# Second feed-forward product in 25 blocks of 128 tokens instead of 32 items of 100

## What is computed

```python
def _qlinear(x, W, b):
    xq, sx, zx = _affine_quantize(x)          # min and max of all of x
    wq, sw = _sym_quantize(W)
    acc = jnp.einsum('bsh,oh->bso', xq - zx, wq)
    return acc * (sx * sw) + b
h = _qlinear(x, W1, b1)                       # 256 -> 1024
h = jax.nn.gelu(h, approximate=False)
out = _qlinear(h, W2, b2)                     # 1024 -> 256
...
x = x + _L0_xattn_ref(_layernorm(x), ctx_1024, ctx_1024, WQ, WK, WV, WO, mask)
x = x + _L0_ffn_ref(_layernorm(x), W1, b1, W2, b2)
```

## Time and profile before

| what | value |
|---|---|
| median of 3 runs | 1148.35 us (1147.01 to 1148.54) |
| the profiled execution, its time | 1149.17 us |
| the profiled execution, its span | 1147.3 us |
| PE busy | 1028.6 us, 90% of the span |
| DVE busy | 984.7 us, 86% |
| ACT busy | 871.5 us, 76% |
| POOL busy | 767.8 us, 67% |
| tail: first matmul of line 1261 to the end of the span | 1113.51 to 1147.3 us |

### The profile page before, as it was taken

One profiled execution on the slowest core, in us unless ns is written; L12 is line 12 of the kernel. 1 busy time (PEld: TensorE's weight loads), 2 busy tenths in 40 slices (PEclk: granted clock), 3 DMA queues, 4 the chain that ended last, 5 costly groups with the idle time before them and its releaser, 6 DMA issues.

```text
span 1147.3 us, 37568 instructions
## 1 busy us (share of the span) xinstructions
PE 1028.6 (90%) x10545; PEld 655.0 (57%) x10545; DVE 984.7 (86%) x2539; ACT 871.5 (76%) x1809; POOL 767.8 (67%) x1103
## 2 busy tenths in 40 slices
PE   4996899999999999999999999999999999975628
PEld 2553466666666666666666666666666666653318
DVE  5775899999999999999999999999999999965987
ACT  4652888888888888888888888888888888855824
POOL 2234677777777777777777777777777777764500
PEclk9998999999999999999999999999999999986959
DMA  8300576666666666666666666666666666664003
GB/s 258 94 1 18 100 136 132 132 133 133 133 133 133 133 133 133 133 133 133 133 132 132 132 132 132 132 132 132 132 132 132 132 132 132 132 128 127 1 0 116
DMA packets 441299, 138.22 MB, mean 120 GB/s; under 512 B 413556, under 2 KB 440252, under 8 KB 441276
## 3 DMA queue, kind: packets, MB, share of 16 engines
q1 hardware_dynamic: 441276, 137.93, 57.5%
HBM read 28.57 MB, written 6.55 MB: 31 GB/s over the span
## 4 chain that ended last, share of the span: by engine, by line
PE 73%; DVE 10%; ACT 6%; issue 4%; POOL 4%; DMA 1%; DVEq 1%; ACTq 0%; SPq 0%; POOLq 0%
PE front L337 18%; PE front L338 16%; PE front L339 16%; PE back L1196 8%; PE front L1178 6%; PE tp L1178 5%; POOL hl L571 3%; DVE hrange L1038 2%; DVE hrange L1039 2%; ACT prob L679 2%; DVE prob L914 2%; PE front L1261 1%; DVE k_l L934 1%; ACT q_h L721 1%; ACT ctx_h L713 1%
## 5 line engine op out<-in xcount | busy, mean ns | idle before, releaser
L571 POOL TENSOR_TENSOR hl<-prob,hl 100x361 f16<-100x361 f32 x512 | 432.7, 855 | 106.2 <-ACT hl L685 54.2
L679 ACT ACTIVATE prob<-prob,nmax 100x361 f32<-100x361 f32 x512 | 293.9, 586 | 46.8 <-DVE nmax L914 46.6
L337 PE MATMUL front<-ctx_h,wk_h 128*128 128x362 f16 x512 | 165.0, 322 | 42.2 <-DVE k_l L934 21.9
L1196 PEld LDWEIGHTS back<-v,pT 128*128 128x128 f16 (+1 forms) x4608 | 165.0, 98 | 45.7 <-issue 9.3
L685 ACT ACTIVATE hl<-prob 100x361 f16<-100x361 f32 x352 | 176.0, 500 | 7.9
L1196 PE MATMUL back<-v,pT 128*128 128x65 f16 (+1 forms) x4608 | 174.1, 194 | 7.0 <-DMA pT<-hl 7.0
L339 PE MATMUL front<-ctx_h,wk_l 128*128 128x362 f16 x512 | 162.4, 317 | 0.0
L338 PE MATMUL front<-ctx_l,wk_h 128*128 128x362 f16 x512 | 162.2, 317 | 0.0
L689 ACT ACTIVATE k_h<-front 128x362 f16<-128x362 f32 x256 | 118.9, 465 | 56.2 <-PE front L339 56.1
L934 DVE SCALAR_TENSOR_TENSOR k_l<-front,k_h 128x362 f16<-128x362 f32 x256 | 135.0, 528 | 27.9 <-ACT k_h L689 25.1
L914 DVE CUSTOM_DVE_ANT_0 prob<-front,mask_g,ngain 100x361 f32<-100x361 f32 x256 | 149.6, 584 | 2.9 <-PE front L1178 0.6
(11 more groups left out here) (180 smaller groups left out, 2011.6 us busy)
## 6 DMA issues: line engine op xcount, KB each, us to landing
ctx_raw<-ctxT SPq DMA_DIRECT2D x33, 361.0 KB, 3.2
pT<-hl SPq DMA_TRANSPOSE x256, 3.6
xs<-x SPq DMA_DIRECT2D x8, 400.0 KB
q_all<-x SPq DMA_DIRECT2D x32, 100.0 KB
out<-q_all SPq DMA_DIRECT2D x32, 100.0 KB
xb<-out SPq DMA_DIRECT2D x8, 400.0 KB
out<-xb SPq DMA_DIRECT2D x32, 100.0 KB
q_all<-wq SPq DMA_DIRECT2D x1, 1024.0 KB, 6.6
```

Of the source, the lines that this page charges most:

```text
L337: eng.matmul(dst, lh, rh, start=first, stop=False)
L571: pool.tensor_tensor(hl[0:T, n % RT, 1, 0:S], prob[0:T, n % RP, 0:S], hl[0:T, n % RT, 0, 0:S], ALU.subtract).then_inc(s_lo, 1)
L679: act.activation(prob[0:T, n % RP, 0:S], prob[0:T, n % RP, 0:S], ACT.Exp, bias=nmax[0:T, n:n + 1], scale=-1.0).then_inc(s_exp, 1)
L1196: ins = pe.matmul(obank[j % 2][:, n % GH * DV:(n % GH + 1) * DV], pT[0:r, n % RT, part_ * ST + st, :], v2[half][0:r, st, v, n % HT, :], st ...
```

## The change

The second product, the residual and the output no longer go item by item. All 3200 tokens are one row, cut into `NT` = 25 blocks of 128 tokens, which cross the boundaries of items.

```diff
+NT = B * T // P
+NX = 5
+CD = 3
-    hq = place("hq", [P, NB, NF, TW], F16)
+    hq = place("hq", [P, NF, B * T], F16)
-    xb2 = place("xb2", [P, B, D], F32)
+    xb2 = place("xb2", [P, NT, D], F32)
+    def blocks_of(c):
+        return [n for n in range(NT) if (n * P + P - 1) // TW == c]
+    def tokens(w):
+        return w.rearrange("b t d -> (b t) d").rearrange("(n p) d -> p n d", p=P)
...
         sp.dma_start(b2r[0:T, :], b2).then_inc(s_b12, 16)
+        sp.dma_start(b2r[T:P, :], b2[0:P - T, :]).then_inc(s_b12, 16)
...
-        for c in range(NB):
-            sp.dma_start(xb2[0:T, c * TB:(c + 1) * TB, :],
-                         out[c * TB:(c + 1) * TB].rearrange("b t d -> t b d")).then_inc(s_xi, 16)
-        for b in range(B):
-            sp.wait_ge(s_o, b + 1)
-            sp.dma_start(out[b], xb2[0:T, b, :]).then_inc(s_out, 16)
+        for c in range(NX):
+            ns = slice(c * NT // NX, (c + 1) * NT // NX)
+            sp.dma_start(xb2[:, ns, :], tokens(out)[:, ns, :]).then_inc(s_xi, 16)
+        for n in range(NT):
+            sp.wait_ge(s_o, n + 1)
+            sp.dma_start(tokens(out)[:, n, :], xb2[:, n, :]).then_inc(s_out, 16)
...
-        for c in range(NB):
-            x1 = xb2[0:T, c * TB:(c + 1) * TB, :]
-            pool.tensor_tensor(x1, x1, b2r[0:T, :].unsqueeze(1).broadcast_to([T, TB, D]), ALU.add).then_inc(s_xb, 1)
+        for c in range(NX):
+            x1 = xb2[:, c * NT // NX:(c + 1) * NT // NX, :]
+            pool.tensor_tensor(x1, x1, b2r[:, :].unsqueeze(1).broadcast_to([P, NT // NX, D]), ALU.add).then_inc(s_xb, 1)
...
-        for c in range(NB):
+        for c in [c for c in range(NB) if c != CD]:
             ts = slice(0, TW // 2 if c == 0 else TW)
-            act.activation(hq[:, c, :, ts].bitcast(I16), hid[:, c, :, ts], ACT.Identity,
+            act.activation(hq[:, :, c * TW + ts.start:c * TW + ts.stop].bitcast(I16), hid[:, c, :, ts], ACT.Identity,
...
-            for b in range(c * TB, (c + 1) * TB):
-                dve.wait_ge(s_f2, b + 1)
-                dve.scalar_tensor_tensor(out=xb2[0:T, b, :], in0=obanks[b % 8][0:T, 0:D], scalar=sc[0:T, S2:S2 + 1],
-                                         in1=xb2[0:T, b, :], op0=ALU.mult, op1=ALU.add).then_inc(s_o, 1)
+            for n in blocks_of(c):
+                dve.wait_ge(s_f2, n + 1)
+                dve.scalar_tensor_tensor(out=xb2[:, n, :], in0=obanks[n % 8][:, 0:D], scalar=sc[:, S2:S2 + 1],
+                                         in1=xb2[:, n, :], op0=ALU.mult, op1=ALU.add).then_inc(s_o, 1)
...
         for c in range(1, NB):
-            dve.wait_ge(s_h1, c + 1)
+            if c == CD:
+                dve.wait_ge(s_hd, 3)
+            else:
+                dve.wait_ge(s_h1, c + 1 - int(c > CD))
             h_codes(c, slice(0, TW))
+            if c == 1:
+                h_ints(CD, slice(0, TW))
             if c >= 2:
                 outputs(c - 2)
...
-                pe.wait_ge(s_hq, i // 2 + 1 if c == 0 else c + 2)
-                if b >= 8:
-                    pe.wait_ge(s_o, b - 7)
-                for m in range(NF):
-                    ins = pe.matmul(obanks[b % 8][0:T, 0:D], hq[:, c, m, i * T:(i + 1) * T], w2q[:, m, :],
+        for n in range(NT):
+            last = n * P + P - 1
+            pe.wait_ge(s_hq, last // TW + 2 if last >= TW // 2 else 1)
+            if n >= 8:
+                pe.wait_ge(s_o, n - 7)
+            for m in range(NF):
+                ins = pe.matmul(obanks[n % 8][:, 0:D], hq[:, m, n * P:(n + 1) * P], w2q[:, m, :],
```

More of the change, by code:

```diff
@@ L495, in _ @@
         sp.wait_ge(s_xo, 16 * B)
-        for c in range(NB):
-            sp.dma_start(xb2[0:T, c * TB:(c + 1) * TB, :],
-                         out[c * TB:(c + 1) * TB].rearrange("b t d -> t b d")).then_inc(s_xi, 16)
-        for b in range(B):
-            sp.wait_ge(s_o, b + 1)
-            sp.dma_start(out[b], xb2[0:T, b, :]).then_inc(s_out, 16)
-        sp.wait_ge(s_out, 16 * B)
+        for c in range(NX):
[4 more added lines that the diff above has]
+            sp.dma_start(tokens(out)[:, n, :], xb2[:, n, :]).then_inc(s_out, 16)
+        sp.wait_ge(s_out, 16 * NT)
     @block.gpsimd
@@ L608, in _ @@
                                ALU.max).then_inc(s_yp, 1)
-        pool.wait_ge(s_b12, 32)
-        pool.wait_ge(s_xi, 16 * NB)
-        for c in range(NB):
-            x1 = xb2[0:T, c * TB:(c + 1) * TB, :]
-            pool.tensor_tensor(x1, x1, b2r[0:T, :].unsqueeze(1).broadcast_to([T, TB, D]), ALU.add).then_inc(s_xb, 1)
+        pool.wait_ge(s_b12, 48)
+        pool.wait_ge(s_xi, 16 * NX)
+        for c in range(NX):
+            x1 = xb2[:, c * NT // NX:(c + 1) * NT // NX, :]
+            pool.tensor_tensor(x1, x1, b2r[:, :].unsqueeze(1).broadcast_to([P, NT // NX, D]), ALU.add).then_inc(s_xb, 1)
     @block.scalar
@@ L1044, in h_codes, with h_ints @@
         def h_codes(c, ts):
-            h = hq[:, c, :, ts]
+            h = hq[:, :, c * TW + ts.start:c * TW + ts.stop]
             dve.tensor_scalar(h, h.bitcast(I16), col(LO2), col(HI2), ALU.max, ALU.min).then_inc(s_hq, 1)
         def outputs(c):
-            for b in range(c * TB, (c + 1) * TB):
-                dve.wait_ge(s_f2, b + 1)
-                dve.scalar_tensor_tensor(out=xb2[0:T, b, :], in0=obanks[b % 8][0:T, 0:D], scalar=sc[0:T, S2:S2 + 1],
-                                         in1=xb2[0:T, b, :], op0=ALU.mult, op1=ALU.add).then_inc(s_o, 1)
+            for n in blocks_of(c):
+                dve.wait_ge(s_f2, n + 1)
+                dve.scalar_tensor_tensor(out=xb2[:, n, :], in0=obanks[n % 8][:, 0:D], scalar=sc[:, S2:S2 + 1],
+                                         in1=xb2[:, n, :], op0=ALU.mult, op1=ALU.add).then_inc(s_o, 1)
         first, second = slice(0, TW // 2), slice(TW // 2, TW)
-        dve.tensor_scalar(hq[:, 0, :, second].bitcast(I16), hid[:, 0, :, second], col(INV2), None,
-                          ALU.mult).then_inc(s_hd, 1)
+        def h_ints(c, ts):
+            dve.tensor_scalar(hq[:, :, c * TW + ts.start:c * TW + ts.stop].bitcast(I16), hid[:, c, :, ts], col(INV2), None,
+                              ALU.mult).then_inc(s_hd, 1)
+        h_ints(0, second)
         dve.wait_ge(s_h1, 1)
@@ L1061, in _ @@
         dve.tensor_tensor(col(S2), col(SPAN), col(SW + 1), ALU.mult).then_inc(s_hd, 1)
-        dve.wait_ge(s_xb, NB)
+        dve.wait_ge(s_xb, NX)
         dve.wait_ge(s_hd, 2)
         for c in range(1, NB):
-            dve.wait_ge(s_h1, c + 1)
+            if c == CD:
+                dve.wait_ge(s_hd, 3)
+            else:
+                dve.wait_ge(s_h1, c + 1 - int(c > CD))
             h_codes(c, slice(0, TW))
+            if c == 1:
+                h_ints(CD, slice(0, TW))
             if c >= 2:
@@ L1253, in _ @@
         top_red(1)
-        for c in range(NB):
-            for i in range(TB):
-                b = c * TB + i
-                pe.wait_ge(s_hq, i // 2 + 1 if c == 0 else c + 2)
-                if b >= 8:
-                    pe.wait_ge(s_o, b - 7)
-                for m in range(NF):
-                    ins = pe.matmul(obanks[b % 8][0:T, 0:D], hq[:, c, m, i * T:(i + 1) * T], w2q[:, m, :],
-                                    start=m == 0, stop=m == NF - 1)
-                ins.then_inc(s_f2, 1)
+        for n in range(NT):
[5 more added lines that the diff above has]
+                ins = pe.matmul(obanks[n % 8][:, 0:D], hq[:, m, n * P:(n + 1) * P], w2q[:, m, :],
+                                start=m == 0, stop=m == NF - 1)
+            ins.then_inc(s_f2, 1)
     block_cm.__exit__(None, None, None)
```

## The result

| | before | changed |
|---|---|---|
| median | 1148.02 us (1147.01 to 1149.22, 6 runs) | 1142.62 us (1139.51 to 1144.15, 6 runs) |
| ratio, 95% interval | | 0.9949 (0.9934 to 0.9964) |
| profiled execution: time, span | 1149.17, 1147.3 us | 1143.48, 1140.9 us |
| start of the last reduction (1108.97) to the start of the last output | 35.45 us | 29.30 us |
| last output's end to the span's end | 2.40 us | 2.15 us |

The change makes the kernel 0.5% faster, 5.4 us by the medians and 6.4 us by the spans of the two profiled executions. Everything up to 1109 us is as it was: the last reduction (`red`, which brings the 32 partial extremes of `hrange` down to two), from which the tail starts, begins at 1108.97 us in both.

The account below looks back on a forecast made before the run. TensorE's second product was taken to bound the tail. From the median, 1148.35 us less 6.1 us for 56 fewer matmuls, with 0 elsewhere, gave 1142.2 us; range 1140.6 to 1144.2 us, its top taking in VectorE at half rate.

Parts of the forecast that it names:

- 56 matmuls fewer at 0.1094 us: TensorE's second product: 200 matmuls replace 256 at an unchanged full-clock pace, saving 6.1 us.
- The pace of 0.107 us: Second product: lower end for the time per matmul, from 256 columns at 0.43 ns; 0.4 us less over 200.
- term of -0.4 us: Allowance in the range for a faster pace of the second product's 200 matmuls.
- The ends of the range: Main case, 1140.6 to 1143.8 us: 1142.2 with -0.4 (pace), +-0.3 (last transfer), +-1 us (clock and scatter).
- The cover of ScalarE and VectorE: Tail: ScalarE done at 1129.7 us, VectorE's codes of chunk 7 at 1131.0 us, 3.8 us ahead of need; cost 0.
- the pass of chunk 3: Int16 codes of chunk 3, moved from ScalarE to VectorE: 1.9 us for 3200 elements, covered by a 1.64 us wait.
- A form of 8 runs of 400 elements: VectorE's codes keep their fast rate; rivals: half rate, 1144.2 us, chance 0.05; VectorE the bound, 1156 us, chance 0.03.
- The moved pass buys nothing: Chunk 3's pass on VectorE gains nothing on the path, only widens ScalarE's cover from 1.1 to about 4 us.
- The last transfer: Outgoing block of 131 KB for 102 KB: taken as 0, within 0.3 us; a skill rule suggested some 0.1 us lower.
- the sign of 2.3 to 2.5 us behind the last output: End of the span: if right, this distance would follow the last output, itself 6.1 us earlier.
- The clock: TensorE's rise to 2.4 GHz, some 5 to 6 us into the second product; other moments allowed 1 us.

Follow-up runs that it names:

- e3: Changed kernel with 100 instead of 128 stationary columns per block, the last 28 tokens left out of product and addition: 1143.37 us, 0.9954 of the kernel before.
- e7: Changed kernel with five added VectorE reductions behind the codes of chunks 2 to 6, 8.65 us of work: 1148.26 us, 0.9995 of the kernel before.
- e6: Changed kernel with two added VectorE reductions behind the codes of chunks 5 and 6, 3.5 us of work: 1143.22 us, 0.9949 of the kernel before.
- e1: Changed kernel with chunk 3's int16 pass given back to ScalarE, blocks alone: 1142.39 us, 0.9948 of the kernel before.
- e2: Kernel before with only chunk 3's int16 pass moved from ScalarE to VectorE, no blocks: 1148.26 us, 0.9998 of the kernel before.
- e5: Changed kernel sending out only the first 100 of each block's 128 rows: 1142.43 us, 0.9947 of the kernel before.
- e8: Changed kernel run again, unaltered, on another chip: 1143.79 us, 0.9946 of the kernel before.
- e11: Changed kernel run a third time, unaltered, on a third chip: 1141.44 us, 0.9939 of the kernel before.
- e4: Changed kernel with unread matmuls added on TensorE in the tail, ahead of the second product: 1140.95 us, 0.9936 of the kernel before.
- e9: Changed kernel with unread matmuls added in the tail and ahead of the first feed-forward product: 1139.08 us, 0.9922 of the kernel before.

## Why the prediction was right

The time was put at 1142.2 us, with 1140.6 to 1144.2; it is 1142.62 us. Step by step:

- *56 matmuls fewer at 0.1094 us.* Measured 224 - 168 at 0.109 us, 6.15 us between the two measures. The pace of 0.107 us that the prediction took as its lower end was a slip: 256 x 0.43 ns is 0.110 us, so that the slope gave no term of -0.4 us. The ends of the range don't follow exactly from its terms either (1140.5 and 1143.5 us, for 1140.6 and 1143.8); the result depends on neither. The inference from the earlier trace rows, that a stationary side of 128 columns streams as fast as one of 100, was drawn from matmuls of other lengths; e3 shows it at this length.
- *The cover of ScalarE and VectorE.* ScalarE's last pass ended at 1110.97 + 18.75 = 1129.7 us, as worked out; the pass of chunk 3 took 1.88 us (1.9 predicted); the codes of chunk 7 ended at 1131.0 us (1131.0), 3.7 us ahead of need (3.8). A form of 8 runs of 400 elements takes the 1.10 to 1.11 us of one run of 3200, which the earlier trace rows had let one expect from the halves of chunk 0. e7 shows that the model of the cover prices an excess rightly, 4.6 us expected and 4.64 to 4.74 us measured, as long as the consumer's clock rises late; in e6 the cover was 3.0 us and not 3.8, because it rose early.
- *The moved pass buys nothing.* e1 and e2 show it from both sides.
- *The last transfer.* Taken as 0 within 0.3 us either way; it gained 0.25 us. The range held it and the value missed it, and so did the sign of 2.3 to 2.5 us behind the last output (2.15 us). The prediction reckoned with bytes at a given rate; e5 shows that fewer bytes land later, which fits the number of engines that share the rows.
- *The clock.* The prediction took the moment of the rise from one trace and allowed 1 us for others. That was the weakest term. The first 32 matmuls took 6.39 (changed), 6.27 (e1), 6.57 (e3), 6.50 (e7), 6.28 (e8) and 6.34 us (e11), but 5.0 us in e6 and 5.01 us in e5, whose product starts at 1114.18 us and whose clock, in stretches of PE, rises close to 1117 us:

```profile
1116.00:1117.00 1.00, 1.00 (x7) 0.52 0.00 0
1117.00:1118.00 1.00, 1.00 (x11) 1.00 0.00 0
```

The changed kernel's runs lie between 1139.51 us at a mean granted clock of 0.974 and 1144.15 us at 0.969, a spread of 4.6 us, which is nearly as much as the gain. In e8, too, the two low runs (1139.77 and 1140.48 us) have 0.973 and 0.975, the four high ones 0.969 to 0.970, as expected there. That the low runs owe their 3 us to this one place is not shown: it gives 1.4 us. The front of the feed-forward stage is no source of scatter in the traces: in all eight profiled executions without added matmuls the first reduction starts 3.9 us behind the first product, and in the six in which the last item's output projection didn't have to wait for a transfer, that product starts 19.9 us behind the projection. The start of this projection, however, lies anywhere between 1029.59 and 1031.19 us. So most of the differences between the traces arise ahead of the feed-forward stage; what makes them there is open.

This limits what the median proves. It lies 0.4 us from the forecast, but the same kernel gave 1143.79 us (e8) and 1141.44 us (e11) on the two other chips, 5.5 and 7.2 us under the kernel before, where 5 to 6.5 us were expected for e11. That the first median came so near is luck; the 6.15 us in the measure are not. That the gain by the medians is 5.4 us (0.9949 is 5.9 us) and 6.4 us by the spans is this scatter, and the part of an execution outside its span, which was 1.87 us in one profiled execution and 2.58 us in the other.

## What to carry to other kernels

When a product is bound by the streamed columns, as here (0.109 us per matmul of 256 with 100 and with 128 stationary columns), the stationary side costs nothing up to 128: cut the stationary axis into full blocks of 128, also across the boundaries of items, and count the matmuls. Before that, recount the cover of every producer against the new, earlier moments of need, and state the cover for the fastest execution of the consumer. A transfer of 128 rows may land sooner than one of 100 (by 0.2 us here). And a product of TensorE that starts on the critical path after a rest, as here after 24 us, can start at half the clock; work that nobody reads, placed in the rest, gave 2.1 of 2.9 + 0.25 us back here, until the next producer was late.

## What the runs showed of the hardware that was not expected

- The recorded load of a stationary operand took 98 ns with 128 columns and 125 ns with 100, in the same kernel otherwise (e3), with no effect on the pace of 0.109 us.
- TensorE's clock rose between about 2.8 us (e5) and 5.9 us (e3) after the product began, by the granted clock, in executions with the same order of work ahead of it, and whether it survives a pause differs: in e4 it stayed at 2.4 GHz over a pause of 2.3 us, in e9 it was at 1.2 GHz from 1111 to 1114 us, 1 us after a pause of the same 2.3 us.
- An outgoing transfer of 131 KB on 128 partitions landed about 0.2 us sooner after its output than one of 102 KB on 100 partitions, with 16 small packets instead of 10.
- SyncE issued these transfers 0.49 us apart where they queued up (e6 and e7), so that the last one left 0.5 us behind its output.
